# Four layers on one core: gamma and beta requested two jobs later in the load queue, up weights split behind the first transposed tiles

## The reference, cut to what matters

```python
# layers 0, 2, 3 (role: one number for each sequence)
h = einsum('bsh,bhk->bsk', x, W_down[role]) + b_down[role]       # 512 -> 256
h = gelu(h, exact)
u = einsum('bsk,bkh->bsh', h, W_up[role]) + b_up[role]           # 256 -> 512
y = x + u
yn = (y - mean(y)) * rsqrt(var(y) + 1e-5)
x = yn * gamma[role] + beta[role]
# layer 1: attention in each sequence, then two gelu MLPs of width 2048, clip(x + ..., 0, 1)
```

## Time and profile before

| | |
|---|---|
| median of 3 runs | 2765.02 us (2763.91 to 2767.8) |
| profiled execution | 2764.27 us, its span 2762.6 us |
| mean granted TensorE clock | 0.961 |
| TensorE busy | 2516.5 us (91%) |
| VectorE busy | 1049.7 us (38%) |
| ScalarE busy | 918.2 us (33%) |
| GpSimd busy | 383.4 us (14%) |

### The profile page before, as it was taken

How to read it: one execution, slowest core, us unless ns; L and a number is a source line. 1 busy time by engine, 2 the same in 40 slices (tenths; PEclk the granted TensorE clock), 3 DMA queues, 4 the chain that set the end, 5 groups by cost and what they waited for, 6 DMA issues and landing times. The chain is left out here.

```text
span 2762.6 us, 29174 instructions
## 1 busy us (share of the span) xinstructions
PE 2516.5 (91%) x11376; PEld 2073.9 (75%) x11376; DVE 1049.7 (38%) x1434; ACT 918.2 (33%) x1242; POOL 383.4 (14%) x294
## 2 busy tenths in 40 slices
PE   5778999999999999999999999989999995868774
PEld 4555788888878888887788888878888884757563
DVE  4445333322343342223333422243342224545545
ACT  3434333322233332223434222234332222433432
POOL 1465000000000000000000000000000001355656
PEclk9979999999999999999999999999999997988887
DMA  4335111021120112112011021021111114321123
GB/s 168 137 122 199 53 46 46 31 76 46 49 89 34 58 46 76 46 46 77 31 46 46 32 95 55 30 77 46 46 46 46 46 46 147 121 92 61 62 92 129
DMA packets 41676, 195.64 MB, mean 71 GB/s; under 512 B 5746, under 2 KB 5746, under 8 KB 24836
## 3 DMA queue, kind: packets, MB, share of 16 engines
q1 hardware_dynamic: 35844, 152.68, 15.8%
q0 software_dynamic: 5760, 41.95, 3.9%
HBM read 163.16 MB, written 31.46 MB: 70 GB/s over the span
## 5 line engine op out<-in xcount | busy, mean ns | idle before, releaser
L1178 DVE TENSOR_TENSOR h_lo<-g,h_hi 128x512 fp32r<-128x512 f32 x256 | 177.4, 693 | 756.2 <-ACT h_hi L1086 756.2
L57 PE MATMUL bank<-h_hi,w_hiB 128*128 128x512 f32 x1152 | 449.2, 390 | 11.7 <-DVE h_lo L1155 11.7
L59 PE MATMUL bank<-h_hi,w_loB 128*128 128x512 f32 x1152 | 448.4, 389 | 0.0
L58 PE MATMUL bank<-h_lo,w_hiB 128*128 128x512 f32 x1152 | 448.2, 389 | 0.0
L1083 ACT ACTIVATE g<-bank,bias_cols 128x512 f32<-128x512 f32 x256 | 176.5, 689 | 630.1 <-PE bank L59 393.3
L59 PE MATMUL bank<-o_hi,w_loA 128*128 128x512 f32 x768 | 298.8, 389 | 0.0
L57 PE MATMUL bank<-o_hi,w_hiA 128*128 128x512 f32 x768 | 298.8, 389 | 0.0
L58 PE MATMUL bank<-o_lo,w_hiA 128*128 128x512 f32 x768 | 298.8, 389 | 0.0
L57 PEld LDWEIGHTS bank<-h_hi,w_hiB 128*128 128x128 f32 x1152 | 216.2, 188 | 58.2 <-issue 6.7
L1025 ACT ACTIVATE w_hiB<-w_raw 128x2048 fp32r<-128x2048 f32 x37 | 71.0, 1919 | 565.5 <-PE bank L59 565.5
L59 PEld LDWEIGHTS bank<-h_hi,w_loB 128*128 128x128 f32 x1152 | 216.3, 188 | 45.2
(11 more groups left out here) (210 smaller groups left out, 4345.5 us busy)
## 6 DMA issues: line engine op xcount, KB each, us to landing
w_raw<-in_units_a SPq DMA_DIRECT2D x32, 1024.0 KB, 4.8
w_raw<-in_units_b SPq DMA_DIRECT2D x32, 1024.0 KB, 4.8
w_raw<-in_units_c SPq DMA_DIRECT2D x16, 1024.0 KB, 4.7
w_raw<-in_w_packed SPq DMA_DIRECT2D x30, 512.0 KB, 7.0
w_raw<-in_rows_packed SPq DMA_DIRECT2D x20, 512.0 KB, 4.5
x_tok<-x SPq DMA_DIRECT2D x16, 512.0 KB, 6.7
x<-stage SPq DMA_DIRECT2D x32, 256.0 KB, 2.9
first_gain<-in_rows_packed SPq DMA_DIRECT2D x10, 512.0 KB, 4.8
```

The lines of the kernel that those rows point to most:

```text
L57: pe.matmul(out, lh, rh, start=(i == 0), stop=False)
L58: pe.matmul(out, lh, rl, start=False, stop=False)
L59: last = pe.matmul(out, ll, rh, start=False, stop=(i == len(terms) - 1))
L1178: v.tensor_tensor(h_lo[:, j, cols(n)], g[q % 2][:], h_hi[:, j, cols(n)].bitcast(F32), ALU.subtract).then_inc(hlo_done, 1)
```

## The change

In SyncE's queue the gain request of job j - 2, and not that of job j, stands in step j, behind the down request of job j + 2; the last two gain requests follow the loop. At the start of a stage, ScalarE copies the two halves of the first transposed tile (xT_hi of job 0) before it splits the up weights and the second job's down weights, and its wait for `rows_lo` moves with them; VectorE makes the two xT_lo before its part of the up splits. No instruction is added or taken away.

```diff
@@ sync engine @@
             for j in range(NJ):
                 if j + 2 < NJ:
                     load_down(j + 2)
-                load_gain(j)
+                if j >= 2:
+                    load_gain(j - 2)
                 if fold and j in ahead:
                     to, of, loaded = fold[0][ahead.index(j)]
                     sp.dma_start(to, of).then_inc(loaded, 16)
                 if NL > 1 and j == 1:
                     for r in range(ROLES, NB):
                         load_up(r)
+            load_gain(NJ - 2)
+            load_gain(NJ - 1)
@@ scalar engine @@
             act.activation(up_rows[0:64, :], raw_rows[0:64, :], ACT.Copy).then_inc(rows_hi, 1)
+            act.wait_ge(rows_lo, 1)
+            for i in range(2):
+                transposed_hi(0, i)
             for r in range(ROLES):
                 split_up(r)
             split_down(1)
-            act.wait_ge(rows_lo, 1)
             act.wait_ge(bias_in, 16)
             act.wait_ge(const_ready, 3)
-            for i in range(2):
-                transposed_hi(0, i)
@@ vector engine @@
              .then_inc(rows_lo, 1)
+            for i in range(2):
+                transposed_lo(0, i)
             for r in range(ROLES):
                 split_up(r)
-            for i in range(2):
-                transposed_lo(0, i)
```

## The result

The changed kernel takes 2621.04 us (median of 4 runs, 2620.1 to 2623.26) against 2764.47 (4 runs, 2758.24 to 2767.8) for the kernel before on the same chip: a ratio of 0.9485, 95% interval 0.9467 to 0.9503. The forecast was 2621. The profiled span fell from 2762.6 to 2618.4 us, by 144.2.

The account below looks back on a forecast made before the run. Both FFN stages were taken as bound by a ring of waits through SyncE's queue. First stage 7.7 + 20.0, last stage 5.5 + 110.35, together 143.6 us off 2764.27, gave 2621 us; range 2607 to 2638 for 8 in 10.

Parts of the forecast that it names:

- The ring: Both FFN stages: SyncE holds down-weight requests behind a gain request awaiting GpSimd's addition; a last-stage turn takes 21.5 us.
- sixteen steps: Last FFN stage, steps 3 to 19: 13.55 us each at TensorE's pace, 216.8 against 327.15 us, gaining 110.35.
- what goes is GpSimd's wait for the moments, 20.0 us: First FFN stage: GpSimd's 5 waits for ScalarE's moments disappear, gaining 20.0 us; bounds down by 4, up by 14.
- the 3.7 bound of the prediction: First stage: five GpSimd powers that no longer meet VectorE's split could return 3.7 us; kept only as a bound.
- a sign of being wrong: First stage: scatters under 20 us apart would show the prediction wrong; about 21.4 us was forecast.
- "nothing": First stage: the cheaper power returns nothing if VectorE's 1.2 us split then stretches a GpSimd multiplication instead.
- 9.9 us behind the shift: First stage: moments come 9.9 us behind GpSimd's shift, in time because GpSimd is occupied for at least 10.8.
- The starts, 7.7 and 5.5: Stage starts: copies before up splits gain 7.7 us in the first (bounds 6, 9.5), 5.5 in the last (3.5, 8).
- A: Last stage: GpSimd becomes the bound; at 14.5 us a step 15 us come back, 2636 us; 12 in 100.
- B: First stage: four scatters land 3 us sooner each, 12 us, giving 2609 us; 10 in 100.
- C: SyncE's queue: down load still held by split wait or older addition; steps near 19 us, 2728 us; 4 in 100.
- D: Last stage: the late gain request becomes the wait; steps of 25 us, about 2810 us; 1 in 100.

Follow-up runs that it names:

- experiments 1 to 4: Changed kernel with: old gain order, 2751.43 us; old start order, 2632.38; gain requests one job later instead of two, 2619.51; gain requests sent by GpSimd, 2641.93.
- experiment 4: Changed kernel with gain requests sent by GpSimd behind its additions instead of by SyncE: 2641.93 us, ratio 0.9556.
- experiment 5: Also named gather_between: changed kernel with the first stage's four waiting gathers moved between GpSimd's multiplications and additions: 2596.62 us, ratio 0.939.
- start_only: Changed kernel with gain requests back in their old place, so only the new order at the stage starts: 2751.43 us, ratio 0.9947.
- gain_one_job: Changed kernel with each gain request one job later in SyncE's queue instead of two: 2619.51 us, ratio 0.9476.
- early_power: Changed kernel with job NJ-2's power and shift between job NJ-3's multiplications and additions at each stage's end: 2617.21 us, ratio 0.9468.
- filler_last: Changed kernel with 28 idle TensorE transposes added at the start of the last stage only: 2619.9 us (single run).
- best_two: Changed kernel with the first stage's waiting gathers between multiplications and additions, and job NJ-2's power early in both tails: 2588.24 us, ratio 0.9357.
- experiment 2: Changed kernel with the old order at the stage starts, so only gain requests two jobs later: 2632.38 us, ratio 0.9525.

## Why the prediction was right, and where only its sum was

**The ring and its sixteen steps: right.** The queue place made the wait (experiments 1 to 4), and with it open TensorE's own pace holds: 13.59 us forecast as 13.55, 110.4 us gained from power to power and 109.7 from moments to moments, forecast as 110.35. That GpSimd fits under it with 0.7 to 1.15 us to spare was right too (1.1 to 1.3 measured in the steps with a gather or a scatter), and experiment 4 shows how near that was.

**The first stage, "what goes is GpSimd's wait for the moments, 20.0 us": the cause right, the term mis-sized, 25.1.** The 20.0 us went. Two things that were left at nothing came on top. The five powers cost 5.5 us together instead of 9.0, since GpSimd now comes to them later than VectorE's split: that is the 3.7 bound of the prediction, 3.5 measured, and no multiplication or addition grew for it (4.66 to 4.79 us). The idle time ahead of the four gathers fell from 30.3 to 26.9, of which 1.9 went back because two of the scatter instructions meet a split and take about 2 us (1.95 in the step above) instead of 1.06: 1.5 net. 20.0 + 3.5 + 1.5 = 25.0. The step was therefore 20.2 us on the mean and not 21.4 (whose own parts add up to 21.3). One of the four, at 19.7 us, even lies under the 20 that the prediction named as a sign of being wrong; its gather waited only 5.86 us for the landing, and its power took 1.05; the mechanism is the forecast one. The price of the power should have been taken at its cheap value, as the prediction's own order of events said that the two no longer meet.

The Trainium skill ("GPSIMD Engine Reference", Specifications) has the SBUF interfaces that GpSimd shares with VectorE as a place of contention with VectorE instructions that have two SBUF inputs. The trace agrees for the power, 1.05 us alone and 1.79 beside the split, and for the scatter instruction, 1.06 and 1.95. The prediction feared for the multiplications (its "nothing"); in the changed kernel no split met one, and in experiment 5, where splits met the additions, VectorE's split grew to 3.23 us and the addition did not.

**"9.9 us behind the shift", so "after that the tail is GpSimd's, as before": wrong, 2.1 us.** Job 7's power waited for its moments:

```profile
186.68 1.04 POOL L638 TENSOR_TENSOR first_columns<-first_columns 128x4 f32<-128x4 f32 x1 [2.11 <-ACT first_columns L489]
```

The moments are 9.9 us behind the shift only while GpSimd sets the pace. In the step after the last late gather, GpSimd no longer holds TensorE, and the moments come at TensorE's pace, 14.6 us apart (171.58 and 186.20), while GpSimd's step without a gather's wait is 12.

**The starts, 7.7 and 5.5: the mechanism right, both terms mis-sized, 3.7 and 7.3.** The order of events was as forecast. 3.7 lies outside the prediction's own bounds for this term, 6 and 9.5. Of the 7.7, 1.4 is that x landed later (transposes at 27.08 instead of 25.67), and 2.5 is lost at the second product, at the lower clock. The prediction named the clock as the bound of this term (6 to 9.5) but looked only for a gain from it. With the same order at the start scatter 0 came at 90.06 (start_only), 88.37 (gain_one_job), 90.13 (gather_between), 85.37 (early_power), 89.99 (filler_last) and 88.09 (best_two): worth 3.7 to 8.7 us by run. In the last stage it went the other way. Its first down product started 5.4 us sooner after the stage's begin, which is the 5.5 of the forecast; but the kernel before had a low stretch in the second product (2358.05 to 2366.58, at a granted clock of 0.83), and the changed one had none there (2325.55 to 2332.76, 1.00): 1.3 us more, and 0.6 in the first product.

**The rivals.** A (GpSimd the bound of the last stage) did not come, by 1.1 us in the steps with the least slack. B (scatters land sooner) came at an eighth of its 12 us, 1.5. C and D are excluded: no w_raw wait is left, and GpSimd nowhere waits for a gain.

## What to carry to other kernels

A queue that issues loads is an in-order engine too: a request that must wait for a late consumer holds every independent one behind it, so order the requests by the time at which each may leave, and one job of distance is enough. When such a ring opens, recompute which engine sets the pace in each stretch by itself, since relations read while one engine sets it ("9.9 us behind the shift") end with it. And put a blocking wait behind work that doesn't need it: the four gathers moved by one instruction group gave 24 us, a sixth of what the change itself gave.

The Trainium skill ("DMA: Bandwidth & Descriptors", Anatomy of one DMA — SWDGE (gpsimd) path) says that a semaphore wait happens on the sequencer that issues the DMA, before dispatch. The section is on transfers sent by GpSimd; here the trace agrees for SyncE's queue, which stood 302.8 us in 15 waits at its gain requests with the down requests behind them, and 131.4 us hung on where the gain requests stood (experiment 2).

## What the runs showed of the hardware

- A power or a scatter instruction of GpSimd that begins inside VectorE's down split ends 0.9 us behind the split (1.79 us instead of 1.04, 1.95 instead of 1.06); a split that begins inside an addition of GpSimd ends 1.1 us behind the addition (3.23 us instead of 1.2). In these cases the one that began first kept its time.
- The same product of the same start code, behind a pause of 3.0 to 3.2 us, ran at a granted clock of 0.65 in one kernel and 1.00 in another. With a sooner landing of x (2 us) this makes 5 us at scatter 0 (90.38 against 85.37). A start of a stage of this kernel is thus not to be forecast closer than some 3 us either way.
- A gain request on GpSimd took 1.9 us of it (1.24 of issue ahead, 0.63 itself); on SyncE it is 0.33 us.
- With TensorE instructions added ahead of the core stage's loop, its three returns had waits of 7.6 to 8.3 us in all. Why stays open.
